# One transformer layer on one core: weight splits, a projection and a few small steps issued in another order

## What is computed

```python
h = patches(x) @ W + b                                   # 576 x 192
q, k, v = split(h @ w_qkv.T)                             # 12 heads of 64
q = q * rsqrt(norm_over_heads(q)); k = k * rsqrt(norm_over_heads(k))
p = softmax(q @ k.T / scale)                             # per image and head, 36 x 36
h1 = layernorm(h + (p @ v) @ w_out.T + b_out)
top2, w = router(h1 @ Wr + br)                           # softmax over the two best logits
gu = h1 @ Wgu + bgu                                      # 8 experts, 2 x 192 each
act = (clip(up) + 1) * gate * sigmoid(1.702 * gate)
h2 = layernorm(h1 + sum_over_top2(w * (act @ Wd + bd)))
```

## Time and profile before

| | value |
|---|---|
| device time, median of 3 runs | 144.47 us (144.03, 144.47, 145.9) |
| the profiled execution's own time | 144.63 us |
| its span in the profile | 142.8 us |
| PE busy | 132.8 us, 93% |
| DVE busy | 101.1 us, 71% |
| POOL busy | 79.5 us, 56% |
| ACT busy | 76.0 us, 53% |

### The profile page before, as it was taken

One profiled execution on the slowest core, in us unless ns is written; L12 is line 12 of the kernel. 1 busy time (PEld: TensorE's weight loads), 2 busy tenths in 40 slices (PEclk: granted clock), 3 DMA queues, 4 the chain that ended last, 5 costly groups with the idle time before them and its releaser, 6 DMA issues. The chain is left out here.

```text
span 142.8 us, 4023 instructions
## 1 busy us (share of the span) xinstructions
PE 132.8 (93%) x1586; PEld 123.6 (87%) x1586; DVE 101.1 (71%) x255; ACT 76.0 (53%) x146; POOL 79.5 (56%) x92
## 2 busy tenths in 40 slices
PE   6999999999999999899999993999999999999950
PEld 2779899998989889899899973999999989999940
DVE  0129589468779598656786895478899786788752
ACT  3057889988933564868544481162422455433621
POOL 7303159670499999998640779166353254334511
PEclk9999999999999999999999997799999999999998
DMA  5999955720121225225810000000000000000021
GB/s 134 328 397 409 398 138 134 220 86 0 35 70 46 83 67 152 62 79 146 313 37 0 0 0 7 0 0 0 0 0 5 0 0 0 7 0 2 0 70 54
DMA packets 5962, 12.42 MB, mean 87 GB/s; under 512 B 888, under 2 KB 2872, under 8 KB 5944
## 3 DMA queue, kind: packets, MB, share of 16 engines
q1 hardware_dynamic: 5944, 12.18, 25.7%
HBM read 9.96 MB, written 0.44 MB: 73 GB/s over the span
## 5 line engine op out<-in xcount | busy, mean ns | idle before, releaser
L482 POOL TENSOR_TENSOR reg_r<-reg_p,reg_r 128x324 fp32r<-128x324 f32 (+1 forms) x23 | 19.0, 829 | 21.9 <-ACT reg_r L712 21.9
L408 POOL TENSOR_TENSOR reg_w<-stage,reg_w 128x768 fp32r<-128x768 f32 x12 | 22.5, 1887 | 6.8 <-ACT reg_w L544 6.7
L712 ACT ACTIVATE reg_r<-reg_p 128x324 fp32r<-128x324 f32 (+1 forms) x24 | 10.7, 444 | 27.6 <-DVE reg_p L1061 27.6
L1061 DVE SCALAR_TENSOR_TENSOR reg_p<-reg_q 128x324 f32<-128x324 f32 (+1 forms) x24 | 15.5, 645 | 2.2
L1038 DVE TENSOR_SCALAR reg_q<-ps,bup 128x324 f32<-128x324 f32 (+1 forms) x24 | 12.3, 511 | 6.7 <-PE ps L1283 6.5
L1279 PE MATMUL ps<-reg_r,reg_w 128*128 128x324 f32 (+1 forms) x48 | 15.1, 315 | 0.0
L1280 PE MATMUL ps<-reg_r,reg_w 128*128 128x324 f32 (+1 forms) x48 | 14.5, 302 | 0.0
L1281 PE MATMUL ps<-reg_r,reg_w 128*128 128x324 f32 (+1 forms) x48 | 14.5, 302 | 0.0
L1282 PE MATMUL ps<-reg_r,reg_w 128*128 128x324 f32 (+1 forms) x48 | 14.4, 300 | 0.0
L1283 PE MATMUL ps<-reg_r,reg_w 128*128 128x324 f32 (+1 forms) x48 | 14.3, 299 | 0.0
L703 ACT ACTIVATE reg_q<-ps,sm 128x324 f32<-128x324 f32 (+1 forms) x24 | 11.7, 489 | 3.3 <-PE ps L1283 3.3
(11 more groups left out here) (196 smaller groups left out, 393.5 us busy)
## 6 DMA issues: line engine op xcount, KB each, us to landing
reg_x<-xw_in SPq DMA_DIRECT2D x5, 416.0 KB, 6.1
stage<-w_gu_a SPq DMA_DIRECT2D x4, 384.0 KB, 4.5
stage<-w_gu_b SPq DMA_DIRECT2D x4, 384.0 KB, 3.4
reg_r<-reg_x SPq DMA_DIRECT2D x24, 54.0 KB
stage<-w_qkv_a SPq DMA_DIRECT2D x3, 384.0 KB, 7.7
stage<-w_qkv_b SPq DMA_DIRECT2D x3, 384.0 KB, 8.2
stage<-w_down SPq DMA_DIRECT2D x3, 384.0 KB, 4.0
wout<-w_out SPq DMA_DIRECT2D x1, 576.0 KB, 10.0
```

Of the source, the lines that this page charges most:

```text
L408: nc.gpsimd.tensor_tensor(dst[:, 1, :], raw, f(dst[:, 0, :]), ALU.subtract).then_inc(s_wlop, 1)
L482: nc.gpsimd.tensor_tensor(acts[:, n % NACT, 1, 0:w], act_f[:, n % 4, 0:w], f(acts[:, n % NACT, 0, 0:w]), ALU.subtract).then_inc(s_alo, 1)
L1061: nc.vector.scalar_tensor_tensor(out=act_f[:, n % 4, 0:w], in0=glu[:, n % 4, 0:w], scalar=GLU_LIMIT, in1=upw[:, n % 4, 0:w], op0=ALU.min, ...
```

## The change

Only calls change places; no instruction is added, and none is removed.

- **PE:** in the turns 4 and 5, `project(k-4)` stands behind `scores(k+1)`, ahead of `weighted(k-2)` and `p_transpose(k-1)`; before it stood behind both.
- **POOL:** `root(0)` and `root(1)` close the turns 4 and 5 (before they opened the turns 5 and 6). Piece 10 moves behind `root(1)`, piece 11 from ahead of `probs(6)` to behind `root(2)`, piece 12 behind `gap_exp(0)`, and `root(3)` from ahead of the pieces 13, 14 and 15 to behind them. The counts on which SP and PE wait for a piece follow the new order by themselves (`LO_ORDER`).
- **ACT:** the high parts of the pieces 13 and 14 are made ahead of `o_evac(7)`, 15 between `expert(0)` and `expert(1)`, 16 behind `expert(1)`. Before, 13 stood behind `expert(0)` and 14, 15, 16 behind `expert(3)`.
- **DVE:** the statistics of the groups 0 and 1 close the turns 4 and 5, which leaves them in the same place among the instructions; `ln1(0)` comes ahead of `row_sum(5)`; `up_in(2)` comes ahead of `ln1(3)`.

```diff
-        LO_ORDER = [2, 3, 4, 5, 6, 7, 8, 9, 11, 10, 12, 13, 14, 15, 16]
+        LO_ORDER = list(range(2, 17))
...
             for k in range(0, NU):
-                if k in (5, 6):
-                    root(k - 5, TSIZES[k - 5], s_ve, s_rstd)
-                if k in (3, 4, 5, 6):
-                    w_lo((7, 8, 9, 11)[k - 3])
+                if k in (3, 4, 5):
+                    w_lo(k + 4)
+                if k == 6:
+                    w_lo(10)
                 probs(k)
                 if k + 3 < NU:
                     k_norm(k + 3)
-                if k == 5:
-                    w_lo(10)
+                if k in (4, 5):
+                    root(k - 4, TSIZES[k - 4], s_ve, s_rstd)
             root(2, TSIZES[2], s_ve, s_rstd)
+            w_lo(11)
+            gap_exp(0)
             w_lo(12)
-            gap_exp(0)
             gap_exp(1)
             gap_exp(2)
-            root(3, TSIZES[3], s_ve, s_rstd)
             w_lo(13)
             w_lo(14)
             w_lo(15)
+            root(3, TSIZES[3], s_ve, s_rstd)
             act_lo(0)
...
             pt_evac(7)
+            w_hi(13)
+            w_hi(14)
             o_evac(7)
             expert(0)
-            w_hi(13)
+            w_hi(15)
             expert(1)
+            w_hi(16)
             w2_hi(0)
             expert(2)
             h1_evac(3)
             expert(3)
-            w_hi(14)
-            w_hi(15)
-            w_hi(16)
             act_hi(0)
...
             for k in range(2, NU):
-                if k in (5, 6):
-                    ln1_stats(k - 5)
-                row_sum(k)
                 if k == 5:
                     ln1(0)
+                row_sum(k)
                 if k + 1 < NU:
                     row_max(k + 1)
...
                 if k in (2, 3, 4):
                     q_norm(k + 3)
+                if k in (4, 5):
+                    ln1_stats(k - 4)
...
             w2_lo(0)
+            up_in(2)
             ln1(3)
-            up_in(2)
...
                 scores(k + 1)
                 if k in (2, 3):
                     v_proj(4, (k - 2,))
+                if k in (4, 5):
+                    project(k - 4)
                 weighted(k - 2)
                 p_transpose(k - 1)
-                if k in (4, 5):
-                    project(k - 4)
```

## The result

| | before | changed |
|---|---|---|
| device time, median of 4 runs | 145.17 us (144.03 to 145.9) | 152.05 us (150.51 to 152.79) |
| ratio, with 95% interval | | 1.045 (1.032 to 1.058) |
| the profiled execution's own time | 144.63 us | 150.51 us |
| its span | 142.8 us | 148.7 us |
| mean granted clock of PE | 0.985 | 0.974 |

The changed kernel is slower by 4.5%. The forecast was 146.4 us, 1.2% slower, with a range up to 148.5; a loss of over 2% had a chance of 0.31. So the direction is the forecast one, and the size lies outside the range. The profile's page of the changed kernel shows where to look: the span's busy times, and the strips of PE and of its clock, one character for each 3.7 us.

The account below looks back on a forecast made before the run. PE was taken as the bound, busy 132.8 of 142.8 us. From the profiled 144.63 us, -4.16 + 2.97 + 2.0 = +0.8 gave 145.4, and +1.0 for the clock gave 146.4 us; range 143.6 to 148.5.

Parts of the forecast that it names:

- step 1: PE's late idle time in down(0) goes and gate_up(4) runs at full clock, so spread(3) starts earlier: -4.16 us.
- Steps 2 and 3: PE idles before project(1), delaying weighted(3) (+1.37), then ACT's exps(6), and PE idles before subtract_max(7) (+1.6): together +2.97 us.
- Step 4: On POOL root(3) comes late behind the pieces, so PE waits at h1_transpose(3): +2.0 us, bounds 1.6 to 2.6.
- Step 5: The remaining moves, such as up_in(2) ahead of ln1(3) and row_sum(5) behind ln1(0), cost nothing.
- Step 6: PE's clock may fall behind the new holes: 0 to +3.0 us, taken as +1.0.
- contention decides: Rival: choose(1), choose(2) and the pieces delay each other; w_transpose(0) and h1_transpose(3) wait, 2.6 us and more; 147.5 us; chance 0.10.

Follow-up runs that it names:

- e1: Kernel before with only PE's order changed: project ahead of weighted and p_transpose in turns 4 and 5; 148.48 us, ratio 1.017.
- e4: Changed kernel, with POOL waiting for the third choose ahead of piece 13; 152.07 us, ratio 1.044.
- e3: Kernel before with only ACT's order changed: high parts of pieces 13 to 16 made early; 142.6 us, ratio 0.981.
- e8: Changed kernel with root(3) moved back ahead of pieces 13, 14 and 15 on POOL; 147.27 us, ratio 1.013.
- e2: Changed kernel with PE's projections back in their old place; 147.73 us, ratio 1.016.
- e10: Changed kernel with one sum over 324 SBUF columns on DVE ahead of group 1's cast in router_weights; one run, 150.47 us.
- e11: Changed kernel with four sums over 324 SBUF columns on DVE ahead of group 1's cast in router_weights; one run, 152.48 us.
- e9: Changed kernel with a 324-column multiplication, both inputs in SBUF, on DVE right ahead of group 1's cast in router_weights; one run, 153.01 us.
- e7: Changed kernel, with POOL waiting for the third choose between pieces 13 and 14; one run, 147.18 us.
- e6: Changed kernel with the two-column cast in router_weights written as two one-column casts; one run, 152.46 us.

## Why the prediction was wrong, point by point

**The bound, and step 1 (-4.16): right.** `down(0)` has no wait in the changed kernel, and `gate_up(4)` runs at full clock behind it (95.48 to 96.96 is 1.48 us). POOL was idle for 4.96 us ahead of `act_lo(0)`, waiting for ACT, so it was not POOL that set its start.

**Steps 2 and 3 (+2.97): right.** `exps(6)` came at 65.33 (forecast 65.25), `row_max(7)` at 66.40 (66.33), `subtract_max(7)` at 67.06 (67.0), and `w_transpose(0)` 3.00 us later than before (80.60 against 77.60). The first hole is shorter than the step said, 1.54 us by the profile and not 2.05, since PE reached it a little later; the second is 1.28 against 1.4. e1 has the two holes with this part alone.

**Step 4 (+2.0, bounds 1.6 to 2.6): this is the step that failed.** It let `choose(1)` and `choose(2)` fall beside the pieces 12 to 14 and sized their trouble by the rows at hand, an `expert_act` of 2.09 us and two `choose` rows of 1.14 us. I took their stretching as what any DVE instruction pays there. It is a wait, and its length depends on when POOL lets the instruction in: the `expert_act` was done at 85.00, so it got in between the pieces 14 and 15 (82.82 to 86.67), and the `choose` rows had one POOL instruction beside them. The cast was let in only at the end of POOL's row, and the row I was moving had 5.5 us in it (78.28 to 83.77). The measured price is 5.35 us at `w_transpose(0)` (86.15 against 80.80), twice the upper bound. The place was wrong too: `root(3)`, the term that the step had computed, cost only 0.25 us at `h1_transpose(3)`, since PE came there later still. The step's sum for POOL was right: the pieces ended at 83.77 (forecast 83.6). But `root(3)` did not follow them. It started at 87.19, after 3.41 us of idle POOL, because its statistics were queued on DVE behind the held cast. With the router set free and the pieces started later, in e4, the wait does come at `h1_transpose(3)`, with 3.89 us.

**Step 5 (nothing): right**, as far as the rows show. No wait for `up_in(2)` or for a late piece appears.

**Step 6 (clock, +1.0): about right in size, for another reason.** The profiled execution has one fall, behind the 3.66 us wait, and it costs 1.7 us (2.85 - 1.48 in `gate_up(2)`, 0.3 behind it). The early holes cost none in it. In executions of other kernels with the same holes they did (below). Why the median, 152.05, lies 1.5 us above the profiled 150.51 isn't shown: of the three other executions two have the same mean clock of 0.974.

By the rows the sum is -4.16 + 2.97 + 5.35 + 1.7 = +5.9, the growth of the span; the 0.25 us at `h1_transpose(3)` and some smaller gains cancel. The rival "contention decides" had the mechanism and the place, at 147.5 us and 1 chance in 10. It was priced as "2.6 us and more", and I worked no upper end out for the "more". Priced by the length of POOL's row, up to 5.5 us in place of the 2.0, the sum would have been 145.4 + 3.5 = 148.9 without the clock, outside my range. No row of the kernel before showed a hold of a whole row of pieces; a run with the pieces beside the router was needed to see it.

## What to carry to other kernels

Before POOL work is moved into a "hole" of POOL, look at what DVE does in that hole: a short DVE instruction with two SBUF inputs, or one that copies more than one element per partition within SBUF, can be held for the whole unbroken row of POOL's instructions, so the price can be the row's length and is not a share of the instruction's own time. Whether it gets in earlier is not predictable from these runs. An instruction that waits (here `root(3)`) may be doing work as a fence, and taking it away costs what it kept out. And try the half of a change that only reorders the producer: ACT's order alone gave 1.9%, and with one piece in a hole where the router was already through it was 2.7% (the two intervals overlap).

## What the runs showed of the hardware

- **DVE behind POOL.** Holds of 5.80, 5.79, 5.66, 5.41, 4.22 and 2.27 us, each of an instruction of some 0.15 us, each ending with the last of POOL's back-to-back instructions. Not held: casts of one element (0.13 and 0.14 us beside piece 12), sums (0.48 us beside piece 13) and `up_in`, which reads PSUM (0.54 us beside piece 15 in e3).
- **A hold does not always last to the end of POOL's row.** The first cast waits 1.15 to 1.17 us for piece 12 and gets in ahead of a `gap_exp` that follows without a gap. The multiplication `q_norm` (432 columns, 0.54 us alone) takes 2.16 us at 50.95 in the kernel before, misses one boundary in a row of POOL and gets in at the next. `expert_act` (324 columns) got in between the pieces 14 and 15 before (2.09 us), in e8 (2.02) and in e3 (0.65), where the casts of the changed kernel, e2, e10 and e11 missed the same boundary; in e9 a cast and the rows behind it got in within the row (1.24 and 2.29 us). Only the smallest instructions were held to the end of a row of pieces, but the first cast and e9 show small ones that got in earlier, and no run varied the size alone. What decides at a boundary stays open.
- **The clock behind short holes is not the same in every execution.** The early holes (1.54 and 1.28 us of idle PE) were followed by no low clock in the changed kernel, e7 and e10, by one behind both in e1, e8 and e9, and by one behind the second alone in e4, e6 and e11. e6 and e11, with the one early fall more, have spans of 150.6 us, where the changed kernel and e10, with waits of the same size and without it, have 148.7 and 148.6. The length of the hole does not settle it: 2.47 us in the profile of the kernel before were followed by the low clock, 2.46 us in e1 and 2.09 us in e7 were not. The kernel before shows the same: 4 of 13 executions had a mean granted clock of 0.998 or more and took 143.04 to 143.47 us; the other nine, at 0.978 to 0.988, took 143.34 to 146.11. So a hole of this length is to be priced with a chance.
